# A fused Mamba and mixture-of-experts kernel: VectorE gates the sums out of PSUM in the first half, GpSimd makes a fourth input product

## What is computed

```python
x = x + attn(cond(x, ids))            # cond: low-rank adapter chosen per sequence, then a layer norm
# attn: four Mamba layers, each on the result of the one before
xz = layer_norm(x) @ Wi.T;  xs, z = split(xz)
u  = silu(conv1d(xs) + cb)            # 4 taps, 256 channels
dt, B, C = split(u @ Wx.T);  dt = softplus(dt @ Wdt.T + bdt)
h[t] = exp(dt[t] * A) * h[t-1] + dt[t] * B[t] * u[t]     # 16 states per channel
y  = sum_over_states(h * C) + u * Dp
x  = x + (y * silu(z)) @ Wo.T
# then: eight dense experts and a shared one for every token (cond2), then a top-2 router
# with a capacity, dispatch, eight expert FFNs (gelu) and the weighted sum back
x = x + ffn(cond2(x))
```

## Time and profile before

| | us |
|---|---|
| median of 3 runs (2601.73 to 2603.53) | 2601.78 |
| the profiled execution | 2602.57 |
| its span | 2600.8 |
| first scan starts | 76.1 |
| one round in the first half (rounds 2 to 12) | 54.5 |
| one round of rounds 16 to 30 | about 64.9 |
| last scan starts | 2014.3 |
| sparse phase, first DMA issue | 2437.8 |

### The profile page before, as it was taken

One profiled execution on the slowest core, in us unless ns is written; L12 is line 12 of the kernel. 1 busy time (PEld: TensorE's weight loads), 2 busy tenths in 40 slices (PEclk: granted clock), 3 DMA queues, 4 the chain that ended last, 5 costly groups with the idle time before them and its releaser, 6 DMA issues. The chain is left out here.

```text
span 2600.8 us, 22792 instructions
## 1 busy us (share of the span) xinstructions
PE 2339.2 (90%) x6094; PEld 1030.8 (40%) x6094; DVE 2047.0 (79%) x2011; ACT 1609.3 (62%) x2605; POOL 2050.7 (79%) x1264
## 2 busy tenths in 40 slices
PE   6688888888898889999999999999997999999994
PEld 4233333333333333333333333333333444444473
DVE  5799999999999999999999999999999243333121
ACT  3576777776777677777777777777775232232131
POOL 4599999999998899999999999999998233221266
PEclk9799999999999999999999999999999999999897
DMA  7455545564445766676667666766675400000533
GB/s 224 186 209 207 190 161 180 208 211 167 143 156 184 255 248 235 236 242 231 242 236 244 238 234 235 246 237 232 234 238 195 136 18 17 29 9 9 154 58 36
DMA packets 216931, 464.97 MB, mean 179 GB/s; under 512 B 29468, under 2 KB 109154, under 8 KB 216802
## 3 DMA queue, kind: packets, MB, share of 16 engines
q1 hardware_dynamic: 204818, 455.30, 51.6%
q0 software_dynamic: 11264, 7.98, 2.0%
q10 hardware_dynamic: 720, 0.23, 0.1%
HBM read 440.00 MB, written 23.99 MB: 178 GB/s over the span
## 5 line engine op out<-in xcount | busy, mean ns | idle before, releaser
L936 DVE TENSOR_TENSOR_SCAN hh<-decays,psdB 128x1024 f32<-128x1024 f32 x512 | 1165.9, 2283 | 62.0 <-ACT decays L736 20.3
L1075 POOL TENSOR_TENSOR products<-hh,Clo 128x1024 f32<-128x1024 f32 x408 | 962.6, 2363 | 94.1 <-DVE hh L936 93.2
L467 PE MATMUL psY<-products,ident 128*128 128x512 f32 x1674 | 824.8, 612 | 104.6 <-POOL products L1075 65.4
L736 ACT ACTIVATE decays<-dt,Acur 128x508 f32<-128x508 f32 x1024 | 667.7, 708 | 6.9 <-DVE hh L936 6.5
L467 PEld LDWEIGHTS psY<-products,ident 128*128 128x128 f32 x1674 | 306.8, 192 | 552.0 <-issue 358.4
L925 DVE TENSOR_TENSOR psdB<-psT,Blo 128x1024 f32<-128x1024 f32 x395 | 484.1, 1226 | 33.1 <-ACT psT L704 7.6
L1505 DVE TENSOR_TENSOR ac<-sg,d_bank 128x512 f32<-128x512 f32 x135 | 92.7, 688 | 222.9 <-PE d_bank L1352 204.2
L447 PE MATMUL psW<-xnT,wcur 128*128 128x512 f32 x496 | 227.5, 601 | 41.6 <-DMA diag<-diags_l 22.7
L1075 POOL TENSOR_TENSOR products<-hh,late 128x1024 f32<-128x1024 f32 x104 | 244.1, 2369 | 19.4 <-PE psY L467 19.4
L1079 POOL TENSOR_TENSOR products<-products 128x512 f32<-128x512 f32 x187 | 237.2, 1269 | 14.7
L1403 ACT ACTIVATE sg<-d_bank 128x512 f32<-128x512 f32 x135 | 80.6, 597 | 243.2 <-PE d_bank L1348 243.1
(11 more groups left out here) (219 smaller groups left out, 3061.8 us busy)
## 6 DMA issues: line engine op xcount, KB each, us to landing
Blo<-rows SPq DMA_DIRECT2D x280, 512.0 KB, 5.9
Clo<-rows SPq DMA_DIRECT2D x280, 512.0 KB, 5.1
late<-rows SPq DMA_DIRECT2D x104, 512.0 KB, 6.1
wcur<-taps_l SPq DMA_DIRECT2D x31, 512.0 KB
fw<-in_Wg SPq DMA_DIRECT2D x36, 256.0 KB, 5.3
fw<-in_Wu SPq DMA_DIRECT2D x36, 256.0 KB, 4.7
fw<-in_Wd SPq DMA_DIRECT2D x36, 256.0 KB, 5.5
disp<-fw SPq DMA_DIRECT2D x16, 528.0 KB, 7.3
```

What stands on the lines that cost most here:

```text
L467: ins = pe.matmul(psY[:, :], lhsT=ident[:, :], rhs=gg[k % NGB][:, j, :], start=False, stop=(k % NK == NK - 1 and j == last - 1))
L736: ins = act.activation(dA[k % NDA][:, j, :, 1:T], dt[i % 2][:, c, :, 1:T], ACT.Exp, scale=Acur[i % 2][:, s:s + 1])
L936: dve.tensor_tensor_scan(out=hh[k % NHB][:, :, :].rearrange("p c t -> p (c t)"), data0=dA[k % NDA][:, :, :, :].rearrange("p c q t -> p (c ...
L1075: ins = pool.tensor_tensor(gg[k % NGB][:, :, :], hh[k % NHB][:, :, :], tile(Clo, Chi, slot(i, s)), ALU.mult)
```

## The change

In rounds 0 to 12 the two `copy_sums` of ScalarE and the two `gate` products of GpSimd are replaced by two VectorE products (new `gate` of VectorE, psY·silu(z) into `yg`): channel half 0 at VectorE's step 12, half 1 at step 4 of the next round. `skip` of TensorE waits for these. GpSimd makes four products instead of three (for steps 4, 8, 11, 14, at its steps 0, 4, 7, 10). For all rounds from the third statistics on, variance + eps and minus the mean are made by ScalarE at its step 10 (`split_moments`), ahead of the copy `turn1` that stands there from round 13 on, and `deviation` keeps two of four operations and moves to step 7. `dtu1` of ScalarE moves from step 1 to step 3. In `PAIRED` 6 takes the place of 7. At the start the first x is loaded ahead of the ids and has its own semaphore, and TensorE does 12 matmuls of 128 columns without a use before it. The 32 matmuls at the end of the dense phase are gone; 20 of 512 columns stand at the head of the sparse phase instead, and SP waits for the first, second and third rows loaded before it issues the next.

```diff
-ACT_AT = {1: ["dtu0", "params", "dtu1", "norm"], 2: ["turn0"], 4: ["sums1", "x0"], 5: ["x1"], 6: ["z0"], 7: ["z1", "silu"], 8: ["bcdt"], 10: ["turn1"], 11: ["dt0"],
+ACT_AT = {1: ["dtu0", "params", "norm"], 2: ["turn0"], 3: ["dtu1"], 4: ["sums1", "x0"], 5: ["x1"], 6: ["z0"], 7: ["z1", "silu"], 8: ["bcdt"], 10: ["moments", "turn1"], 11: ["dt0"],
           12: ["dt1", "sums0", "softplus"], 13: ["outT"], 14: ["added"], 15: ["centre"]}
-GIVEN = {4: 0, 9: 5, 13: 8}
-POOL_AT = {1: ["gate1"], 6: ["rstd"], 10: ["dt"], 11: ["dtu"], 12: ["gate0"]}
+GIVEN = {4: 0, 8: 4, 11: 7, 14: 10}
+POOL_AT = {1: ["gate1"], 7: ["rstd"], 10: ["dt"], 11: ["dtu"], 12: ["gate0"]}
-PAIRED = [0, 2, 3, 4, 5, 7, 8, 9, 13, 14, 15]
+PAIRED = [0, 2, 3, 4, 5, 6, 8, 9, 13, 14, 15]
...
                 sp.dma_start(ids[:, :], A["ids"]).then_inc(ids_ld, 16)
+                sp.dma_start(xg[0], A["x"][0:G].rearrange("b t d -> t b d")).then_inc(x0_ld, 16)
                 sp.wait_ge(ids_ld, 16)
...
                 def skip(i, c):
-                    at_least(pe, ycopied, NH * i + c)
+                    if NH * i + c <= NH * RING0:
+                        at_least(pe, ygated, NH * i + c)
+                    else:
+                        pe.wait_ge(ycopied, NH * (i - RING0) + c)
...
                 pe.wait_ge(cst, 1)
+                for r in range(12):
+                    pe.matmul(psW[:, 0:128], lhsT=ident[:, :], rhs=ident[:, :], start=True, stop=True)
...
+                def split_moments(t):
+                    act.wait_ge(moments, t + 1)
+                    act.wait_ge(rstd_ok, t)
+                    act.activation(vare[:, :], mv[:, :, 1], ACT.Identity, bias=K["eps"][:, 0:1])
+                    act.activation(negm[:, :], mv[:, :, 0], ACT.Copy, scale=-1.0).then_inc(rs, 1)
...
+                def gate(i, c):
+                    dve.wait_ge(red, NSTEP * i + NK * (c + 1))
+                    if i > 1:
+                        dve.wait_ge(wready, W["out", i - 2] + 1)
+                    dve.tensor_tensor(yg[i % 2][:, c, :], psY[:, :], sz[i % 2][:, c, :], ALU.mult).then_inc(ygated, 1)
...
+                        if k == 4 and 0 < i <= RING0:
+                            gate(i - 1, 1)
+                        if k == 12 and i < RING0:
+                            gate(i, 0)
                         input_term(i, k)
...
-                pe.wait_ge(silued, CR + NST * NDT)
-                for r in range(32):
-                    pe.matmul(psG[r % 2][:, :], lhsT=ident[:, :], rhs=wgu[:, 0, 0, :], start=True, stop=True)
...
+                for r in range(20):
+                    pe.matmul(psT[0][:, :], lhsT=K["ident"][:, :], rhs=K["fw"][:, 0, :], start=True, stop=True)
                 turn(0, 0)
```

More of the change, by code:

```diff
@@ L211, in wave_phase @@
             sem("a_" + n) for n in "xT_up xT_ok hid_up hid_ok cond_up cond_ok stats_ok var_ok rs h_ok neg".split())
-        a_st, pch, half_ln, half_dt, half_dtu = (sem(n) for n in "a_st pch half_ln half_dt half_dtu".split())
+        a_st, pch, half_ln, half_dt, half_dtu, x0_ld = (sem(n) for n in "a_st pch half_ln half_dt half_dtu x0_ld".split())
         ad_ld = [sem(f"ad_ld{p}") for p in range(NAB)]
@@ L245, in at_least, with rows_of @@
                 eng.wait_ge(sm, v)
+        def rows_of(g):
+            return 16 * (1 + G) * (g // NAB + 1) - (16 if g % NAB == 0 else 0)
         def residents(d):
@@ L272, in load_adapter @@
                     at_least(sp, h_ok, g + 1 - NAB)
-                    sp.dma_start(xg[p], A["x"][G * g:G * (g + 1)].rearrange("b t d -> t b d")).then_inc(ad_ld[p], 16)
+                    if g > 0:
+                        sp.dma_start(xg[p], A["x"][G * g:G * (g + 1)].rearrange("b t d -> t b d")).then_inc(ad_ld[p], 16)
                     for q in range(G):
@@ L404, in turn_x @@
                     p = g % NAB
-                    pe.wait_ge(ad_ld[p], 16 * (1 + G) * (g // NAB + 1))
+                    if g == 0:
+                        pe.wait_ge(x0_ld, 16)
+                    else:
+                        pe.wait_ge(ad_ld[p], rows_of(g))
                     at_least(pe, xT_ok, g - 1)
@@ L413, in hidden @@
                     pe.wait_ge(xT_ok, g + 1)
+                    if g == 0:
+                        pe.wait_ge(ad_ld[p], rows_of(0))
                     at_least(pe, hid_ok, g)
@@ L836, in _ @@
                                 act.preload_act_table_set(LNEXP)
+                            if what == "moments" and i + 2 < NIT:
+                                split_moments(i + 2)
                             if what == "centre" and i + 2 < NIT:
@@ L842, in _ @@
                                 added(i - 1)
-                            if what == "sums1" and i > 0:
+                            if what == "sums1" and i > RING0:
                                 copy_sums(i - 1, 1)
-                            if what == "sums0":
+                            if what == "sums0" and i >= RING0:
                                 copy_sums(i, 0)
@@ L948, in statistics @@
                     dve.wait_ge(stat, t + 1)
+                    at_least(dve, rs, 2 * t - 1)
                     at_least(dve, centred, t)
@@ L1039, in deviation @@
                 def deviation(t):
-                    pool.wait_ge(moments, t + 1)
                     at_least(pool, centred, t)
-                    pool.tensor_tensor(vare[:, :], mv[:, :, 1], K["eps"][:, :], ALU.add)
-                    pool.tensor_scalar(negm[:, :], mv[:, :, 0], -1.0, None, ALU.mult).then_inc(rs, 1)
+                    if t < 2:
+                        pool.wait_ge(moments, t + 1)
+                        pool.tensor_tensor(vare[:, :], mv[:, :, 1], K["eps"][:, :], ALU.add)
+                        pool.tensor_scalar(negm[:, :], mv[:, :, 0], -1.0, None, ALU.mult).then_inc(rs, 1)
                     pool.wait_ge(rs, 2 * t + 1)
@@ L1116, in _ @@
                         for what in POOL_AT.get(k, ()):
-                            if what == "gate1" and i > 0:
+                            if what == "gate1" and i > RING0:
                                 gate(i - 1, 1)
-                            if what == "gate0":
+                            if what == "gate0" and i >= RING0:
                                 gate(i, 0)
@@ L1564, in load_rows @@
                             sp.dma_start(dx[c][e][:, 0:HC, :], A["disp"][c, e, 0:CAP // NHT].rearrange("(n p) d -> p n d", p=128)).then_inc(x_first, 16)
+                        sp.wait_ge(x_first, 32)
                     for c in range(2):
@@ L1574, in _ @@
                 for e in range(NE):
+                    if 0 < e < 3:
+                        sp.wait_ge(x_ld[BATCH[e - 1]], 32)
                     load_rows(e)
```

3 lines of the change are left out of this document (2 added, 1 removed).

## The result

The changed kernel takes 2623.31 us (median of 4 runs), the kernel before 2601.76: a ratio of 1.0090, 95% interval 1.0077 to 1.0103. It is slower, as forecast, but by 21.5 us and not by 7; the time lies 2 us above the top of the range. The profiled execution took 2622.42, with a span of 2620.7 against 2600.8: 19.9 more.

The account below looks back on a forecast made before the run. No single engine bounded the kernel: a loop through all engines closed the 54.52 us round. Terms -0.5 - 0.8 + 11.3 + 1.6 + 2.5 - 6.3 = +7.8 gave 2609 us, range 2583 to 2621.

Parts of the forecast that it names:

- 0.3 behind the last engine, as before: Barrier: without the 32 matmuls the sparse phase starts at about 2419.6; part of a total gain of 6.3 us.
- The round: First half: scan 8, gate of step 4, skip, z1, ScalarE's decays and move, next scan 8; 55.55 us.
- Both holds: First half: step 4's gate delays skip, z1 and scan 8; step 12's delays skip, out and scan 14 by 0.6.
- VectorE alone sets the round: Rival, first half: gates hold nobody, the round is 53.2 us and the time 2583; chance 0.17.
- I take 1.03: First half: each round becomes 1.03 us longer; over eleven rounds, 2 to 12, +11.3 us.
- 0.4 more: Round 12 into 13: 0.4 us beyond the 0.6 hold, within the +1.6 that includes round 13's extra VectorE gate.
- Two small operations leave it: First half, GpSimd: moving two small operations to ScalarE saves it 0.1 + 0.4 us a round; GpSimd bounds nothing.
- The other two steps: Barrier: forty matmul records take 20.1 us; the stretch after them runs at 2.4 GHz, gaining 3.6 us.
- The start: Up to scan 8 of round 0: x load ahead of the ids gains 0.5 us, an earlier move 0.8.
- the 0.8 of round 0: Round 0: scan 8 comes 0.8 us sooner because ScalarE's move of its product is earlier.
- The slow side's 2620: Rival, first half: TensorE idles before both skips and its clock falls, 1 us in each of eleven rounds; chance 0.13.
- The rule on SBUF: VectorE's gates could stand behind a GpSimd product of 2.4 us, making rounds 57 us or more; given nothing.

Follow-up runs that it names:

- the last run: Changed kernel with both gates one step earlier, four filler matmuls per first-half round, 5 barrier dummies, moments on GpSimd from round 13: 2589.96 us, ratio 0.9953.

## Why the prediction was wrong, and where it was right

The time lies outside the range, above all by the barrier: the step "0.3 behind the last engine, as before" failed, since the sparse phase starts 5.6 us behind GpSimd's last scatter. The second failure is the size of the first half.

- **The round (right).** 55.55 predicted, 55.63 measured, by the loop described: the gate of step 4 starts 39.3 us behind scan 8 (714.23; 38.7 + 0.6 predicted), `skip` follows it, scan 8 of the next round comes 55.63 behind. Both holds were shown by taking them away: 0.59 us with the gate at step 11, and 0.8 more with both gates early (55.04 to 54.2). The 1.95 of the shortest rounds with the gate at step 3 is more than the hold is worth in a steady round. The rival "VectorE alone sets the round", 53.2, isn't reached even with both gates early.
- **Rounds 1 to 12 (term too small: 11.3 for 14.0).** The step that failed is "I take 1.03": it holds for a round at 2.4 GHz (1.11 measured). The eleven rounds lost 15.5, and the 14.0 are that less 1.5 gained between scan 8 of round 0 and of round 1 (56.56 to 55.04), for which no term stood. The idle time ahead of both `skip`s was named, but only as a rival of 0.13, at 1 us a round. It came smaller: in the changed kernel scan 14 waits 3.0 us longer over the twelve rounds. The other 1.3 of the 4.3 above 667.6 are the wait at scan 0 of round 13 below and a gap of 0.4 that VectorE has once in the kernel before too. With the gate alone it is 13.9 of 15.3 (682.9 over 667.6). What a low stretch costs depends on where it falls: in these two runs 1.7 us, once 2.1, on the z matmuls or ahead of out, 0 to 0.4 elsewhere; 2.6 to 2.9 where, with the moments back, it began at 12 us and lasted 6.8.
- **Rounds 12 and 13 (1.6 for 3.2).** The step "0.4 more" missed two waits of VectorE for ScalarE's copy of a turned half, 0.9 at scan 0 of round 13 and 1.0 at its scan 8. They are there with the gate alone too (4.50 us between scans 15 and 0) and gone without it (3.74). The first of them:

```profile
812.80 1.23 DVE L949 TENSOR_TENSOR psdB<-psT,Blo 128x1024 f32<-128x1024 f32 x1 [0.90 <-ACT psT L726]
```

- **The moments (size right, effect missed).** 2.5 predicted for the second half, 2.7 measured, on and off. That the same edit shortens the first half, by 22 us, no step of the prediction had. "Two small operations leave it" was put at nothing.
- **The barrier (failed by 5.0 us).** The failing step is "Without them the sparse phase starts at about 2419.6 (0.3 behind the last engine, as before)". The 0.3 was read where TensorE came last, with GpSimd's scatters long done. It is 5.6 where GpSimd's scatters come last, since GpSimd's DRAIN ends only 5.3 us behind the issue. The other two steps held: 20.1 us for the forty records predicted, 19.1 measured to the first transposes, and 3.6 gained on the up matmuls, 3.4 measured.
- **The dense phase (0 for 2.0).** The changed kernel has one more stretch at the low clock there (2057.5, 3.4 us, so 1.7 lost); what sets it off wasn't tried.
- **The start (-1.3 for -1.2)** agrees by luck: the first scan's place varies by up to 5 us between executions, and it moved by 1.1 where 0.5 was predicted, while the 0.8 of round 0 did not come (41.3 us from its scan 0 to scan 8, 41.4 before).
- **The slow side's 2620** lies near the measured time, but by luck: of its 11 us for the clock 3.0 came, and the barrier made up the rest.
- The rule on SBUF (a gate held behind a GpSimd product) was rightly given nothing: the gates' rows are 0.67.

So the sum missed by 5.0 (barrier), 2.7 (rounds 1 to 12), 1.6 (the end of the first half), 2.0 (dense phase) and 0.5 (second half), together 11.8 of the 12.1 us by which the span grew more than the 7.8 of the sum.

## What to carry to other kernels

Where a handed-over job moves into an in-order list, read when its turn comes and not how long it takes: both gates together cost VectorE 1.2 us and relieved GpSimd of 2.5, yet one step earlier for both was worth 1.4 us a round (55.63 to 54.2). When a wait for another engine appears ahead of TensorE's matmuls, price it twice, once as the wait and once as the low clock that may follow it on the path. And before removing work that "only holds a barrier", find what else the barrier waits for; it may be hidden under that work.

## What was not expected of the hardware

- A barrier behind GpSimd's indirect DMAs opens 5.6 us after the last one's issue, in all twelve kernels without the 32 matmuls (2440.27 to 2445.87, 2418.22 to 2423.83). GpSimd's DRAIN ends 5.3 us behind the issue in all fourteen traces, the kernel before included. The last scatter's data had landed by then: 1.3 us behind its issue in the kernel before (2420.60). What the DRAIN waits for isn't shown.
- After 18 us of idling, TensorE's forty records began at 0.50 and were at 1.00 after 3.8 us. Five matmuls did as well as twenty.
- Four useless matmuls in 54 us removed all low stretches of twelve rounds, six before; in the last run PE is busy 51.2 of 54.2 us. With the gates early this gained 3 us in all, with the moments back, where seven stretches stayed, 12.3: the clock is one wait among several.
- The upper level of the granted clock was 0.95 through a whole execution of one kernel, and 1.00 in the thirteen other traces.
- The releaser in a row can be the wrong one of two that end within 0.05 us, here a product that the scan did not need.
